# Two-layer recurrent and attention model on one core: the order of TensorE's scores and transposes within a batch is rewritten

## The reference, cut to what matters

```python
xn = _layernorm(x, axis=-1)
q = concat(q_nope, apply_rope(q_rope))           # per head
c_kv = c_kv * rsqrt(mean(c_kv**2) + eps) * kv_norm_w
scores = einsum('bqhd,bkhd->bhqk', q, k) * scale  # causal mask, softmax
out = einsum('bhqk,bkhd->bqhd', attn, v).reshape(B, S, H * V_DIM) @ Wo
g = _silu(x @ base_w.T + base_b + SCALING * lora(x, gate))
x = x + out * g
```

## Time and profile before

| | |
|---|---|
| median of three runs | 797.14 us |
| the profiled execution | 797.71 us |
| its span | 795.9 us |
| TensorE busy | 780.1 us (98%) |
| VectorE, ScalarE, GpSimd busy | 682.7, 524.0, 477.1 us |
| granted TensorE clock | 0.996 of full speed over the span |

### The profile page before, as it was taken

One profiled execution on the slowest core, in us unless ns is written; L12 is line 12 of the kernel. 1 busy time (PEld: TensorE's weight loads), 2 busy tenths in 40 slices (PEclk: granted clock), 3 DMA queues, 4 the chain that ended last, 5 costly groups with the idle time before them and its releaser, 6 DMA issues.

```text
span 795.9 us, 23134 instructions
## 1 busy us (share of the span) xinstructions
PE 780.1 (98%) x7976; PEld 712.7 (90%) x7976; DVE 682.7 (86%) x2615; ACT 524.0 (66%) x1612; POOL 477.1 (60%) x1261
## 2 busy tenths in 40 slices
PE   7999999999999999999999999999999999999988
PEld 5888888888889889899988999999899998999867
DVE  6898797887788799899898998988899998999885
ACT  4554455455563787777767777777777767777682
POOL 6833022022334687776868677686776868668673
PEclk8999999999999999999999999999999999999999
DMA  8600011000001322232222322222232222322120
GB/s 297 251 20 18 1 68 67 1 1 1 1 12 33 55 46 44 55 63 39 52 39 44 56 54 54 38 47 46 54 65 34 49 42 50 57 47 52 33 52 28
DMA packets 101334, 41.15 MB, mean 52 GB/s; under 512 B 91744, under 2 KB 98400, under 8 KB 100576
## 3 DMA queue, kind: packets, MB, share of 16 engines
q1 hardware_dynamic: 98896, 38.89, 21.9%
q10 hardware_dynamic: 2320, 0.79, 0.4%
HBM read 14.47 MB, written 4.19 MB: 23 GB/s over the span
## 4 chain that ended last, share of the span: by engine, by line
PE 88%; DVE 5%; POOL 2%; issue 2%; ACT 2%; ACTq 0%; DMA 0%; POOLq 0%; DVEq 0%
PE bank L537 61%; PE bank L745 11%; PE bank L767 8%; PE bank L738 3%; PE bank L601 1%; POOL par L1822 1%; DVE SM L1583 1%; PE bank L653 1%; ACT SM L1036 1%; PE bank L554 1%; DVE PT L1606 1%; PE bank L613 1%; PE bank L627 1%; POOL SM L1989 1%; PE bank L672 0%
## 5 line engine op out<-in xcount | busy, mean ns | idle before, releaser
L1036 ACT ACTIVATE SM<-SM,stb 128x224 f32<-128x224 f32 (+7 forms) x512 | 206.1, 405 | 63.4 <-DVE stb L1583 58.9
L1989 POOL TENSOR_SCALAR SM<-SM,stb 128x224 f32<-128x224 f32 (+7 forms) x512 | 196.1, 402 | 67.0 <-DVE stb L1590 65.5
L537 PE MATMUL bank<-yh,wq_lo 128*128 128x256 f32 x512 | 150.5, 294 | 0.0
L537 PE MATMUL bank<-yh,wq_hi 128*128 128x256 f32 x512 | 144.6, 282 | 0.0
L537 PE MATMUL bank<-yl,wq_hi 128*128 128x256 f32 x512 | 144.6, 282 | 0.0
L745 PE MATMUL bank<-KT,QT 128*128 128x192 f32 (+4 forms) x640 | 120.9, 327 | 1.7 <-DVE stb L1583 1.7
L1583 DVE CUSTOM_DVE_ANT_0 SM<-bank,CONST 128x224 f32<-128x224 f32 (+3 forms) x320 | 96.9, 346 | 24.1 <-PE bank L745 21.3
L1606 DVE STREAM_TRANSPOSE PT<-SM 128x128 f32<-128x128 f32 (+2 forms) x232 | 99.4, 460 | 16.2 <-PE bank L767 16.2
L745 PEld LDWEIGHTS bank<-KT,QT 128*128 128x128 f32 x640 | 97.5, 190 | 5.3 <-DVE stb L1583 3.6
L537 PEld LDWEIGHTS bank<-yh,wq_lo 128*128 128x128 f32 x512 | 97.0, 190 | 1.4
L537 PEld LDWEIGHTS bank<-yh,wq_hi 128*128 128x128 f32 x512 | 97.0, 190 | 0.0
(11 more groups left out here) (218 smaller groups left out, 2068.9 us busy)
## 6 DMA issues: line engine op xcount, KB each, us to landing
QT<-QA SPq DMA_DIRECT2D x240, 64.0 KB, 2.1
PT<-KV SPq DMA_DIRECT2D x256, 16.0 KB, 1.8
out<-fo SPq DMA_DIRECT2D x32, 128.0 KB, 2.0
X<-in_x SPq DMA_DIRECT2D x7, 512.0 KB, 11.2
stage<-in_wqn SPq DMA_DIRECT2D x2, 1024.0 KB, 9.2
stage<-in_wo SPq DMA_DIRECT2D x2, 1024.0 KB, 5.0
stage<-in_w1t SPq DMA_DIRECT2D x4, 256.0 KB, 5.6
stage<-in_w2t SPq DMA_DIRECT2D x2, 512.0 KB, 7.6
```

The source lines that it names most:

```text
L537: i = e.matmul(dst, a, b, start=(first and j == 0), stop=(last and j == 2), skip_group_check=skip)
L1036: i = e.activation(M[:, at], M[:, at], ACT.Exp, bias=S[:, 0, j:j + 1], scale=-1.0, accum_out=S[:, 1, j:j + 1])
L1989: i = e.tensor_scalar(P[:, at], P[:, at], S[:, 2, j:j + 1], 1.0, ALU.mult, ALU.mult)
```

## The change

For batches 1 to 14, S1 is issued one step later, ahead of S2; S8 one step sooner, behind S7; TY and TM move ahead of Q5; TK moves from step 8 to step 7, behind S8 (in batch 0 it stays); MI1 moves ahead of S9 (in batch 0 as well). In batch 0, TY also moves ahead of Q5, and TM keeps its place. ScalarE's `keys` follows TK one step after it, so it too comes a step sooner. The places in the ring follow the new order. No instruction is added, removed or changed in size. The steady batch becomes:

```diff
-TURN_AT, TM_AT, TK_AT, LORA_AT, MISC_AT = 6, 6, 8, 8, (8, 9)
+TURN_AT, TM_AT, TK_AT, TK_FIRST, LORA_AT, MISC_AT = 6, 6, 7, 8, 8, (8, 9)
...
+def scores_at(n):
+    if not 0 <= n < TOTAL:
+        return ()
+    b, m = divmod(n, UNITS)
+    if 0 < b < NB - 1:
+        return {1: (), 2: (n - 1, n), 5: (n, n + 1), 6: (), 7: (n, n + 1), 8: ()}.get(m, (n,))
+    if n and with_next(n - 1):
+        return ()
+    return (n, n + 1) if with_next(n) else (n,)
+
+def tk_of(n):
+    b, m = divmod(n, UNITS)
+    return b + 1 if m == (TK_AT if b else TK_FIRST) and b + 1 < NB else None
...
 # shared_bank_order
+        if m == TURN_AT and b + 2 < NB:
+            js.append(("ty", b + 2))
+        if m == TM_AT and b and b + 1 < NB:
+            js.append(("tm", b + 1))
         js += [("q", u) for u in Q0_AT.get(n, ())]
         if b + 1 < NB:
             js += [("q", 8 * (b + 1) + u) for u in queries_at(b + 1, m)]
-        if m == TK_AT and b + 1 < NB:
-            js.append(("tk", b + 1))
-        if m == TURN_AT and b + 2 < NB:
-            js.append(("ty", b + 2))
+        if tk_of(n):
+            js.append(("tk", tk_of(n)))
...
-        if m == TM_AT and b + 1 < NB:
-            js.append(("tm", b + 1))
+        if n == TM_AT:
+            js.append(("tm", 1))
...
 # TensorE's loop
+                if m == TURN_AT and b + 2 < NB:
+                    free_shared("ty", b + 2)
+                    l1_turn(b + 2, jof("ty", b + 2))
+                if m == TM_AT and b and b + 1 < NB:
+                    free_shared("tm", b + 1)
+                    l1_tm(b + 1, jof("tm", b + 1))
                 for u in Q0_AT.get(n, ()):
                     l1_q(0, u)
                 if b + 1 < NB:
                     for u in queries_at(b + 1, m):
                         l1_q(b + 1, u)
-                if n < TOTAL and not (n and with_next(n - 1)):
-                    l1_s(n)
-                    if with_next(n):
-                        l1_s(n + 1)
...
+                if m == MISC_AT[1] and b + 2 < NB:
+                    free_shared("mi", 2 * (b + 2) + 1)
+                    l1_misc(b + 2, 1, jof("mi", 2 * (b + 2) + 1))
+                for i in scores_at(n):
+                    l1_s(i)
+                if tk_of(n):
+                    free_shared("tk", tk_of(n))
+                    l1_tk(tk_of(n), jof("tk", tk_of(n)))
+                if m == MISC_AT[0] and b + 2 < NB:
+                    free_shared("mi", 2 * (b + 2))
+                    l1_misc(b + 2, 0, jof("mi", 2 * (b + 2)))
+                if n == TM_AT:
+                    free_shared("tm", 1)
+                    l1_tm(1, jof("tm", 1))
...
 # ScalarE's loop
-                c, i = divmod(n - 1, UNITS)
-                if 0 <= c < NB - 1 and i == TK_AT:
-                    keys(c + 1, jof("tk", c + 1))
+                if n and tk_of(n - 1):
+                    keys(tk_of(n - 1), jof("tk", tk_of(n - 1)))
```

## The result

The changed kernel takes 811.62 us in the median of four runs (811.35 to 811.80); the kernel before, run beside it, 797.25. The ratio is 1.0175, with a 95% interval of 1.0163 to 1.0188: 14.4 us slower. The profiled execution has a span of 809.7 us. The forecast was 809.5 us, slower, between 803.5 and 816.

What follows compares the result with a forecast made beforehand. TensorE, its instructions laid end to end, was taken to bound the kernel. Q5's 9.75 us plus PV's 2.6 less 0 for joining made 12.35, on a median of 797.14: 809.5 us, range 803.5 to 816.

Steps and rivals of the forecast that it cites:

- TensorE laid end to end: Steady batches: TensorE's instructions fill the whole 33.9 us, so every new wait on TensorE is lost in full.
- Joining gives nothing: Ends of single-precision runs, three a batch, 42 in all: removing them gains 0, at most 8.0 us.
- Q5 meets the ring: Q5, now six places behind v0, waits for VectorE's third evacuation after PV: 0.75 us in batches 1 to 13, 9.75 us.
- The release: In Q5's wait: VectorE's third of four evacuations, which frees v0, was taken as over at 507.15 us.
- the restart: In Q5's wait: 0.15 us from the evacuation's end until Q5 starts, weight load included.
- The sign that I had named: In the trace, 340 to 740 us: weight loads waiting on VectorE's evacuation (L1628), 13 times, 0.6 to 0.9 us each.
- PV meets VectorE: Later S9 and S1 make VectorE's last turn late for PV: 0.2 us in batches 2 to 14, 2.6 us.
- What costs nothing: Other moved work (TM, S8, TK, `keys`, LO, MI0, MI1, SP-queue moves): waits hidden or absent, 0 us.
- That joining pays: Rival: each end really costs 0.19 us and v0 is released in time, 789.1 us; chance 0.07 for faster.
- That PV alone doesn't stall: Rival: VectorE catches up during TensorE's new pause, so only Q5's wait counts, 806.9 us; chance 0.2.
- That the delays feed each other: Rival: late S1, VectorE, PV, evacuation, GpSimd or moves add another 0.5 us a batch, 816 us; chance 0.14.
- The rival of gaining ends with a binding ring: Rival: Q5 waits in the ring, but removed ends gain 8.0 us, giving 801.5 us; chance 0.07.

Runs made afterwards that it cites:

- experiment 6: Changed kernel with Q5 issued ahead of TY and TM again and TK's old place in the ring, so the ring order of before: 800.51 us, ratio 1.0038.
- Experiment 9: Kernel of experiment 6 with MI1 behind S9 as before, leaving S1 late as the only change that can delay VectorE: 801.56 us, ratio 1.0052.
- Experiments 1: Changed kernel with Q5 ahead of TY and TM again, in TensorE's order and in the ring's: 809.19 us, ratio 1.0147.
- 4: Kernel before with only S8 and TK moved to step 7, TK ahead of O1 in the ring, keys a step sooner: 806.34 us, ratio 1.0113.
- 8: Changed kernel with TY, then Q5, then TM; S1 at step 1; TK's old ring place behind LO; MI1 still ahead of S9: 811.56 us, ratio 1.0176.
- experiment 7: Kernel before with, in batches 1 to 13, Q1 issued between S0 and S1 and Q0 between S3 and S4: 797.44 us, ratio 0.9996.
- experiments 11: The edit of experiment 8 with the ring ordered ty q5 tm o0 q7 o1 tk lo: 800.21 us, ratio 1.0041.
- 12: As experiment 11, but with MI1 behind S9 again: 796.58 us, ratio 0.9995.

## Why the prediction was right

**TensorE laid end to end.** Right, and it is what made the rest countable: every wait on TensorE came out in the total at its full length. 13 batches times 1.10 us are 14.3 of 14.4.

**Joining gives nothing.** Right. I took 0 with an upper bound of 0.19 us an end. Taking one run away gave a ratio of 0.9998 and adding two gave 0.9996; the bound is now 0.02. The reading by distances of starts, not by drawn lengths, was the one that held. What the Trainium skill says in "TensorE: Matmul & The Clock Gate", in its step-by-step part, of weight loads pulled ahead under running matmuls agrees with these runs. By the section on LDWEIGHTS of the same page of the Trainium skill, exposed loads of 107 ns at 26 added ends would have cost 2.8 us, an estimate; the measured interval ends at 0.4.

**Q5 meets the ring.** Right in mechanism and batches, and a little small: 0.86 us between the changed kernel and experiment 6, 0.87 in the timeline, where the sum had 0.75. The evacuation ends as far behind PV as before. I set two things too low. The release: the third difference was over at 507.20 before, not 507.15. And the restart, for which I had 0.15 us: the weights go in from 513.24, 0.12 after the end at 513.12, with another 0.10 to the matmul. The missing 0.11 us make 1.4 us of the 2.1 by which the total was short. The sign that I had named came in another form: the matmuls name the evacuation (L1651), but the weight loads name ScalarE's copy (L1073), with 0.6 us each.

**PV meets VectorE.** Right: 0.25 us for 0.20, which makes the other 0.65 us. VectorE was paced by S1 (it waits 0.22 us for it, I had 0.26), and from that reading to the last turn's end are 5.41 us (I had 5.37). Experiment 9 adds what the prediction didn't say: MI1 is not part of the price once S1 is late.

**What costs nothing.** GpSimd's product was late for TM, whose weights went in 0.28 us late, and Q5's wait hid it, as worked out. S8 and TK met no wait in the changed kernel, and no wait of TensorE is put down to `keys`. The slack that I left VectorE before S9, 1.12 us, came out at 1.97, which changed nothing in the sum. I had written that TK's ring place is free and had not said why O1, which TK displaces there, is: it has TY six before it. Experiments 1, 4 and 8 show how narrow that is; whoever puts TY or Q5 back meets some 0.65 to 0.85 us a batch.

**The rivals.** That joining pays is excluded by experiment 7. That PV alone doesn't stall is excluded by the trace. That the delays feed each other didn't happen: the thirteen batches take 34.98 to 35.07 us each. The rival of gaining ends with a binding ring fell with the first.

## What to carry to other kernels

On an engine that is full, a new order of the same work can only lose unless the order itself had a price, so measure that price first, by adding what you mean to take away. Where results share a ring of buffers, write down for every job which job stands n places before it, before and after the edit, and when that one is read; a job that isn't touched can get a new neighbour. An engine that was served early may keep another one on time: ask who reads what you now deliver later, and what it delivers in turn.

## What the runs showed that I had not expected

The first evacuation of VectorE isn't set by VectorE: taking 0.7 us of work from in front of it moved nothing, because ScalarE's copy of 0.6 us lay beside that work. And two delays of VectorE need not add up: with S1 late alone PV loses 0.24 us a batch, and with MI1 ahead of S9 as well it loses the same 0.24, since VectorE then idles a microsecond longer before S9 and 0.8 less before S1 (experiments 9 and 6). But MI1 ahead of S9 alone, with S1 at step 1, cost 0.28 us too, at a bank of scores in place of PV (experiments 11 and 12: 800.21 less 796.58, over 13 batches).
